# A two-layer graph network on one core: weight turned in the first linear, degree sums on VectorE, self part emptied by two engines

## What is computed

```python
deg     = segment_sum(ones, dst);  deg_inv = 1 / max(deg, 1)
mean(h) = segment_sum(h[src], dst) * deg_inv[:, None]
h   = relu(x @ W_self0 + mean(x) @ W_neigh0 + b0)
u   = h @ W_self1 + mean(h) @ W_neigh1 + b1
y   = layernorm(x + u)
# GCN: edges (row=src, col=dst) plus one self loop per node
g   = y @ W.T + b;   d = degree(row) ** -0.5
out = layernorm(y + segment_sum((d[row] * d[col])[:, None] * g[col], row))
```

## Time and profile before

| | |
|---|---|
| time, median of 3 runs | 850.34 us (850.06 to 852.06) |
| profiled execution, its own time | 849.59 us |
| its span, first to last instruction | 847.9 us, so 1.7 us lie around it |
| mean granted TensorE clock | 0.999 |
| TensorE busy | 830.6 us, 98% of the span |
| GpSimd busy | 459.1 us, to about 622 us |
| VectorE busy | 461.3 us |
| ScalarE busy | 177.4 us |
| DMA | 180.52 MB, 213 GB/s on average |

### The profile page before, as it was taken

How to read it: one execution, slowest core, us unless ns; L and a number is a source line. 1 busy time by engine, 2 the same in 40 slices (tenths; PEclk the granted TensorE clock), 3 DMA queues, 4 the chain that set the end, 5 groups by cost and what they waited for, 6 DMA issues and landing times.

```text
span 847.9 us, 11000 instructions
## 1 busy us (share of the span) xinstructions
PE 830.6 (98%) x4295; PEld 707.9 (83%) x4295; DVE 461.3 (54%) x714; ACT 177.4 (21%) x218; POOL 459.1 (54%) x343
## 2 busy tenths in 40 slices
PE   8999999999999999999999999999999999999996
PEld 6888888888897899788888888778889889988885
DVE  6465568200017565897544677775556435455555
ACT  4111132110111113353123112222222122200000
POOL 5028887787777887885888788788620000000000
PEclk9999999999999999999999999999999999999999
DMA  9977965463776425668876668267877649555551
GB/s 332 380 304 267 350 193 168 125 176 75 213 236 180 122 57 133 249 237 286 298 282 222 243 220 284 62 176 214 240 245 255 223 150 295 189 199 199 198 193 46
DMA packets 99480, 180.52 MB, mean 213 GB/s; under 512 B 15474, under 2 KB 75898, under 8 KB 94048
## 3 DMA queue, kind: packets, MB, share of 16 engines
q1 hardware_dynamic: 60144, 124.17, 44.0%
q10 hardware_dynamic: 26896, 40.65, 13.3%
q0 software_dynamic: 12384, 14.95, 7.6%
HBM read 107.08 MB, written 72.43 MB: 212 GB/s over the span
## 4 chain that ended last, share of the span: by engine, by line
PE 61%; POOL 15%; DMA 9%; issue 8%; DVE 5%; SPq 1%; ACT 1%; POOLq 0%; ACTq 0%; DVEq 0%
PE ps L1572 19%; POOL adj_in L643 14%; PE ps L1429 12%; PE ps L1606 10%; PE ps L1589 9%; PE ps L1515 8%; DMA adj_in<-u 4%; DMA first_rows<-in_L_gnn_W_neigh 1%; DMA spare<-in_x 1%; DMA xin<-s0t_scr 1%; PE ps L1413 1%; DVE u L914 1%; PE ps L1380 1%; SPq L514 1%; DVE sacc L1303 0%
## 5 line engine op out<-in xcount | busy, mean ns | idle before, releaser
L643 POOL DMA_INDIRECT adj_out<-loops,idx_out x160 | 245.2, 1533 | 65.4 <-issue 65.4
L643 POOL DMA_INDIRECT adj_in<-mult,idx_in x160 | 198.1, 1238 | 86.8 <-issue 86.8
L1572 PE MATMUL ps<-u 128*128 128x512 f32 x840 | 190.7, 389 | 1.4 <-DVE u L914 1.4
L1572 PEld LDWEIGHTS ps<-u 128*128 128x128 f32 x840 | 157.6, 188 | 34.2 <-issue 1.6
L1484 PE MATMUL ps<-wx 128*128 128x512 f32 (+1 forms) x576 | 109.4, 351 | 1.3 <-ACT outb L761 1.3
L1484 PEld LDWEIGHTS ps<-wx 128*128 128x128 f32 x576 | 93.9, 189 | 16.9 <-ACT outb L761 1.9
L1429 PE MATMUL ps<-u 128*128 128x512 f32 x432 | 98.2, 389 | 0.0
L1515 PE MATMUL ps<-wx,u 128*128 128x256 f32 (+5 forms) x640 | 94.8, 309 | 1.2 <-DVE ht L1191 1.2
L1589 PE MATMUL ps<-u,panel_tiles 128*128 128x512 f32 (+1 forms) x400 | 93.9, 393 | 1.9 <-DVE u L914 1.9
L1429 PEld LDWEIGHTS ps<-u 128*128 128x128 f32 x432 | 81.0, 188 | 16.8
L1515 PEld LDWEIGHTS ps<-wx,u 128*128 128x128 f32 (+1 forms) x640 | 86.6, 191 | 8.2 <-DVE ht L1191 1.6
(11 more groups left out here) (167 smaller groups left out, 779.8 us busy)
## 6 DMA issues: line engine op xcount, KB each, us to landing
left_scr<-u SPq DMA_DIRECT2D x7, 2560.0 KB, 9.5
u<-left_scr SPq DMA_DIRECT2D x7, 2560.0 KB, 9.6
xt_scr<-wx ACTq DMA_DIRECT2D x10, 1024.0 KB, 9.9
u<-xt_scr SPq DMA_DIRECT2D x10, 1024.0 KB, 5.1
wx<-xt_scr SPq DMA_DIRECT2D x16, 512.0 KB, 4.0
adj_in<-u POOLq DMA_DIRECT2D x4, 1600.0 KB, 25.3
adj_out<-u POOLq DMA_DIRECT2D x4, 1600.0 KB, 16.1
wx<-adj_in SPq DMA_DIRECT2D x5, 1280.0 KB, 7.1
```

What stands on the lines that cost most here:

```text
L643: pool.indirect_dma_start(table, bass.IndirectOffsetOnAxis(ap=index[0:EP, j:j + 1], axis=0), counts[0:EP, j:j + 1], None, bounds_check=CEL ...
L1572: ins = nc.tensor.matmul(ps[:, product_bank(g, i, p), :], left_op[n % 2][:, p, k, left, :], right_op[n % 2][:, k, right, :], start=(not on ...
```

## The change

1. The GCN weight is turned in the first linear: after steps 10 and 18 of tiles 5 to 8 instead of in mean1. Its loads stand in SyncE's queue between the loads of x tiles 6 to 9, its copies and stores in ScalarE's before the eviction of the tile. The loads of W_self0's first four row blocks then wait for the turning and for the stores.
2. The degrees of mean0's chunks 0 and 1: VectorE sums the 10 panels elementwise (`colsum`), and TensorE needs one matmul against ones instead of ten. It is issued after block 0 of chunk 0 and after block 3 of chunk 1. Chunks 2 and 3 keep theirs.
3. The tiny matmuls of L1522 go. The inverse degrees go through DRAM (dinv_scr): four small stores, one load before mean1.
4. Self part: ScalarE empties the even blocks, VectorE the odd ones, into 8 places; ScalarE issues all stores. The fetches of blocks 0 to 3 are issued during the last chunk of the self part.
5. The tables are cleared from a run of zeros that is a quarter as long, read four times, so four times as many pieces; adj_out is cleared after the first put. Some semaphores are merged, and b1 is loaded after mean0's last degrees.

```diff
@@ SyncE
             for t in range(2, NT):
                 load_x(t)
+                if t in (6, 7, 8, 9):
+                    for k in (2 * t - 12, 2 * t - 11):
+                        sp.wait_ge(w_lo_done, KD * S0)
+                        if k >= 2:
+                            sp.wait_ge(wt_turned, k - 1)
+                        sp.dma_start(raw[:, k % 2, :], w_gcn[k * P:(k + 1) * P, :]).then_inc(wt_in[k % 2], 16)
             for k in range(4):
-                sp.wait_ge(w_lo_done, KD * S0)
+                if k < 2:
+                    sp.wait_ge(wt_turned, 7 + k)
+                else:
+                    sp.wait_ge(wt_stored[k % 2], 16 * KD // 2)
                 load_w(S0, k)
...
+                if i == 20:
+                    sp.wait_ge(xt_turned, NT)
+                    for m in range(4):
+                        fetch_self(m)
...
+                if d == 6:
+                    t0, n = CHUNKS[c]
+                    sp.wait_ge(dinv_row_done, c + 1)
+                    sp.dma_start(dinv_scr[lines(CHUNKS[c])].rearrange("(a j) -> a j", a=1), dinv_row[0:1, c % 2, 0:n * T]
+                                 ).then_inc(dinv_stored[c % 2], 16)
...
@@ GpSimd
-                runs = table.rearrange("(p a j) o -> a p (j o)", a=4, j=ZERO_RUN)
+                runs = table.rearrange("(p a i j) o -> a p i (j o)", a=4, i=ZERO_TIMES, j=ZERO_RUN)
                 for a in range(4):
-                    pool.dma_start(runs[a, :, :], zeros).then_inc(done, 16)
+                    pool.dma_start(runs[a, :, :, :], zeros.unsqueeze(1).broadcast_to([P, ZERO_TIMES, ZERO_RUN])).then_inc(done, 16)
...
-                        if (g, c) == (0, RUN // 2) and not general_form:
+                        if (g, c) == (0, 0) and not general_form:
                             clear(adj_out, cleared_out)
...
@@ ScalarE
+            def keep_turned(k):
+                act.wait_ge(wt_turned, k + 1)
+                if k >= 2:
+                    act.wait_ge(wt_stored[k % 2], 16 * (k // 2))
+                else:
+                    act.wait_ge(w_lo_done, KD * S0)
+                nc.scalar.activation(outb[:, k % 2, :], pair_bank(3), ACT.Copy).then_inc(wt_copied, 1)
...
-            for i, (c, d) in enumerate(S0_BLOCKS):
+            for i, (c, d) in list(enumerate(S0_BLOCKS))[0::2]:
...
-                nc.scalar.activation(staged[i % 4][:, 0:width], ps[:, d, 0:width], ACT.Identity, bias=b0c[:, d:d + 1]).then_inc(s0_free, 1)
+                nc.scalar.activation(staged[i % 8][:, 0:width], ps[:, d, 0:width], ACT.Identity, bias=b0c[:, d:d + 1]).then_inc(s0_free[0], 1)
...
@@ VectorE
+            for i, (c, d) in list(enumerate(S0_BLOCKS))[1::2]:
+                dve.wait_ge(s0_full, i + 1)
...
+                nc.vector.tensor_scalar(staged[i % 8][:, 0:width], ps[:, d, 0:width], b0c[:, d:d + 1], None, ALU.add).then_inc(s0_free[1], 1)
...
                 if d == 0:
+                    if c < 2:
+                        dve.wait_ge(m1_full[c], 16 * n // 2)
+                        nc.vector.tensor_reduce(sacc[:, 0:width].rearrange("p (n j) -> p n j", n=n // 2),
+                                                m1_panels[c][:, :, :, :].bitcast(F32).rearrange("p k n j -> p n j k"), AX_X, ALU.add
+                                                ).then_inc(colsum_done, 1)
+                        dve.wait_ge(colsum_done, 2 * c + 1)
+                        nc.vector.tensor_copy(colsum[:, 0:width], sacc[:, 0:width]).then_inc(colsum_done, 1)
                     dve.wait_ge(deg_full, c + 1)
...
@@ TensorE
+                    if q == N0 and t in WEIGHT_TILES and i in (10, 18):
+                        turn_weights(2 * t - 10 + (i == 18))
...
+            def degrees(c, width, exact):
+                pe.wait_ge(*s0_bank_free(6 + c))
+                pe.wait_ge(colsum_done, 2 * c + 2)
...
+                    ins = nc.tensor.matmul(bank, ones_r[:, :], colsum[:, 0:width], start=True, stop=True)
+                ins.then_inc(deg_full, 1)
...
-                        if d == 2:
-                            pe.wait_ge(dinv_row_done, c + 1)
-                            for i in range(n):
-                                ins = nc.tensor.matmul(ps[:, 6 + c % 2, i:i + 1], dinv_row[0:1, c % 2, i * T:(i + 1) * T],
-                                                       ones_nt[0:1, 0:1], start=True, stop=True)
-                            ins.then_inc(dcol_full, 1)
+                        if (c, d) in ((0, 0), (1, 3)):
+                            degrees(c, width, exact)
...
-                        if 1 <= t <= KD:
-                            turn_weights(t - 1)
```

More of the change, by code:

```diff
@@ L92, in build @@
         base = -(-nc.sbuf_base // 32) * 32
[L93 removed]
+        U_AT, WX_AT, R_AT, E_AT, B_AT, END = (base + n for n in (0, 81920, 163840, 188416, 197120, 201216))
         sb("arena", [P, (END - base) // 4], F32)
@@ L213, in quarter @@
             return buf.rearrange("p a d -> p (a d)")[:, j * BANK:j * BANK + WIDE]
-        staged = [quarter(outb[:, :, :], j) for j in range(4)]
+        staged = [quarter(buf, j) for buf in (outb[:, :, :], raw[:, :, :]) for j in range(4)]
         fetched = [quarter(xin[:, :, :], j) for j in range(4)]
@@ L457, in load_chunk_1 @@
                     sp.wait_ge(h_full, KD * (c - 1))
-                    sp.wait_ge(dsum_done, sum(n for _, n in CHUNKS[:c - 1]) // 2)
+                    sp.wait_ge(dsum_done, sum(n for _, n in CHUNKS[:c - 1]))
                 for b in range(c + 1):
@@ L524, in _ @@
             for j in range(4):
-                sp.wait_ge(s0_stored[j], 16 * 6)
+                sp.wait_ge(s0_stored[j], 16 * 3)
             load_block(0, 1, 0)
+            for s in range(2):
+                sp.wait_ge(dinv_stored[s], 16 * 2)
+            sp.dma_start(dinv[:, :], dinv_scr.rearrange("(t p) -> p t", p=P), allow_slow_non_contiguous=True).then_inc(dinv_in, 16)
+            sp.wait_ge(deg_full, 4)
+            sp.dma_start(bias[:, :], b1.rearrange("(a d) -> a d", a=1).broadcast_to([P, D])).then_inc(bias_full, 16)
             sp.wait_ge(h_sum, KD * 4)
@@ L566, in _ @@
             sp.dma_start(bias[:, :], b_gcn.rearrange("(a d) -> a d", a=1).broadcast_to([P, D])).then_inc(bias_full, 16)
-            for s in range(2):
-                sp.wait_ge(wt_stored[s], 16 * KD // 2)
             load_w(GCN, 0)
@@ L1375, in turn_weights @@
                 if c == 0:
-                    pe.wait_ge(*summed(1, 6, 2))
+                    pe.wait_ge(flag_ready, 1)
+                    pe.wait_ge(b0c_ready, 1)
                 else:
@@ L1492, in typed @@
                 return ap.bitcast(F32) if exact else ap
+            def degrees(c, width, exact):
+                pe.wait_ge(*s0_bank_free(6 + c))
+                pe.wait_ge(colsum_done, 2 * c + 2)
+                bank = ps[:, 6 + c % 2, 0:width]
+                if exact:
+                    ins = nc.tensor.matmul(bank, ones_r[:, :].bitcast(F32), sacc[:, 0:width], start=True, stop=True)
+                else:
+                    ins = nc.tensor.matmul(bank, ones_r[:, :], colsum[:, 0:width], start=True, stop=True)
+                ins.then_inc(deg_full, 1)
             def mean0(exact):
@@ L1498, in mean0 @@
                     pe.wait_ge(m1_full[c], 16 * n // 2)
-                    if c < 2:
-                        pe.wait_ge(s0_free, s0_bank_free(6 + c))
-                    else:
-                        pe.wait_ge(dcol_read, c - 1)
-                    for k in range(NT):
-                        ins = nc.tensor.matmul(ps[:, 6 + c % 2, 0:width].rearrange("p (n j) -> p n j", n=n // 2), typed(ones_r[0:rows(k), :], exact),
-                                               typed(panels[0:rows(k), k, :, :], exact), start=(k == 0), stop=(k == NT - 1))
-                    ins.then_inc(deg_full, 1)
+                    if c >= 2:
+                        pe.wait_ge(deg_read, c - 1)
+                        for k in range(NT):
+                            ins = nc.tensor.matmul(ps[:, 6 + c % 2, 0:width].rearrange("p (n j) -> p n j", n=n // 2),
+                                                   typed(ones_r[0:rows(k), :], exact), typed(panels[0:rows(k), k, :, :], exact),
+                                                   start=(k == 0), stop=(k == NT - 1))
+                        ins.then_inc(deg_full, 1)
                     for d in range(KD):
```

128 lines of the change are left out of this document (64 added, 64 removed).

## The result

| | before | after |
|---|---|---|
| time, median us (8 runs each, side by side) | 851.29 | 857.57 |
| ratio of times | | 1.0091, 95% interval 1.0076 to 1.0106 |
| profiled execution: span us, mean granted clock | 847.9, 0.999 | 855.5, 0.991 |

What follows compares the result with a forecast made beforehand. TensorE, 98% busy, was taken as the bound. Its terms sum to -10.1 us, but new waits and GpSimd's chain leave the gather 2.1 earlier; less 0.2 for the clock, -1.9 on 850.34 gives 848.4 us, range 844.0 to 855.0.

Steps and rivals of the forecast that it cites:

- The savings on TensorE: Work and waits removed from TensorE in mean1, self part, degrees and tiny matmuls: 8.1, 1.3, 1.1 + 3.4 and 2.5 us.
- the chain of GpSimd: Puts, last panel load and gather: the gather starts at 633.2, against 632.9 by TensorE, hiding 0.3 us of clock loss.
- Mean1 and turning in mean1: Mean1 without turning the weight takes 92.0 us instead of 100.1: a gain of 8.1.
- Self part: TensorE's waits for banks that come free late in the self part go: a gain of 1.3 us.
- Third new wait: Before mean0's chunk 2: panels load late behind chunk 1's late degree and VectorE's sums, 5.2 us, bounds 3 and 8.
- Turning in the first linear: Eight groups of transposes moved into the first linear, 0.79 us each: 6.3 us more on TensorE.
- 1 us of wait before the self part: Self part's first loads stand behind the last turned block's store: 1 us late, bounds 0 and 8.
- First new wait: After block 0 of mean0's chunk 0, TensorE waits for VectorE's degree sum: 1.5 us, bounds 0 and 3.
- The clock: Slower TensorE clock after the wait at chunk 2: possible cost 0 to 2 us, taken as 0.2 net.
- Nothing before the products: No change forecast in TensorE's wait between mean0 and the products.
- GpSimd's last put: Last put, gating the gather, moves 2.5 us later through slower clears, with -3 and +11.3 as ends.
- savings 7.0 forecast: In mean0: degrees of chunk 0 (1.1 us) and chunk 1 (3.4), and tiny matmuls removed (2.5).

Runs made afterwards that it cites:

- the second pair: The unaltered kernels before and after, run and profiled once more: 850.25 us beside the after run's 856.66, ratio of after 1.0074.
- r_after: The changed kernel again, unaltered: 856.66 us, ratio 1.0074 to the kernel before.
- e1: Changed kernel with the degrees of chunks 0 and 1 summed by TensorE's ten matmuls again, on a slower chip: ratio 0.9958 to the kernel before.
- e10: Changed kernel with chunk 2's panels asked for before block 12's self part is fetched: 851.39 us, ratio 0.9999 to the kernel before.
- r_before: The kernel before again, unaltered: 849.8 us, ratio 0.9992.
- e9: Changed kernel with 16 filler matmuls in TensorE's wait for chunk 0's degree: 851.29 us, ratio 1.0024 to the kernel before.
- e13: Changed kernel with turning back in mean1, chunk 0's degrees on TensorE, chunk 2's panels asked for earlier, clears as before: 849.03 us, ratio 0.9995 to the kernel before.
- e12: Kernel before with the change's self part alone, clears as before: 847.23 us, ratio 0.9974 to the kernel before.
- e14: Changed kernel with chunk 0's degrees on TensorE, chunk 2's panels asked for earlier, clears as before: 852.73 us, ratio 1.004 to the kernel before.
- e11: Changed kernel with the two clears as in the kernel before: 864.51 us, ratio 1.0175 to the kernel before.
- e16: Kernel before with the changed self part, clears as before, and reciprocal roots brought into columns by memory, on a slower chip: ratio 0.994 to the kernel before.
- e7: Changed kernel with turning back in mean1, chunk 0's degrees on TensorE, chunk 2's panels asked for earlier: 854.5 us, ratio 1.0061 to the kernel before.
- e15: Kernel before with the changed self part, clears in long pieces, the second after the first put, on a slower chip: ratio 0.9992 to the kernel before.
- e6: Changed kernel with the tiny matmuls for the reciprocal roots back: 858.43 us, ratio 1.0082 to the kernel before.
- e2: Changed kernel with chunk 2's panels asked for before the fetch of block 12, on a slower chip: ratio 0.9944 to the kernel before.
- e5: Changed kernel with chunk 0's degrees on TensorE and chunk 2's panels asked for earlier: 850.86 us, ratio 0.9986 to the kernel before.

## Why the prediction was wrong

The savings on TensorE came out as forecast. What failed are prices: turning in the first linear (7.3 with its wait, measured 9.5), the strided sum behind the first wait (1.5 us of wait, measured 4.4), the clock (0.2, measured about 5), and the chain of GpSimd that should have hidden part of it and hid nothing. Term by term:

- **Mean1 and turning in mean1, -8.1**: right (-8.2). **Self part, -1.3**: right (-1.0; 2.2 to 2.4 in the second pair).
- **Third new wait, 5.2 before chunk 2**: right in cause and size (4.8; 5.2 in r_after). e1 and e10 take it away from either side.
- **Turning in the first linear, +6.3, with 1 us of wait before the self part**: mis-sized. A group of transposes costs (13.60 - 11.79) / 2 = 0.91 us, not the 0.79 between two starts, which left out its last overlap: 7.2. With 0.8 of wait for ScalarE's store, 0.7 before the self part and 0.4 from the first tiles, it makes 9.2 of the 9.55 measured. The wait before the self part was right.
- **First new wait, chunk 0's degree, 1.5**: failed at "reads 2560 elements, as the reduction of 2.81 us does". The strided sum took 4.52, and the wait was 4.4, past my upper bound of 3. The sum explains 1.7 of the 2.9 that I missed. Most of the rest is VectorE's start: 1.9 us after block 0's first matmul (247.88 - 245.95), where I had 0.5, because its last self block came late; in e10 it started 0.6 after, and the wait was 3.15. The Trainium skill (SBUF — State Buffer, Door 1: The DMA port swizzle) says that consecutive accesses within one line of 16 bytes run at full rate and each crossing pays; the row above is in line with it, 1.6 times the contiguous one; no run separates the stride from the number of results, 256 a partition instead of 10.
- **The clock, "I take 0.2 net"**: failed. Chunk 2 took 335.49 - 313.12 = 22.4 us, against 321.73 - 300.62 - 0.5 of tiny matmuls = 20.6 in r_before: 1.8. Chunk 0 cost 1.5 (e9). The products, 192.3 from first matmul to last against 190.7 in r_before: 1.6. Together about 5 us in the profiled execution, of which 1.1 comes off again before mean1 (0.82 of wait there instead of 1.94). I had weighed only the wait at chunk 2, at 0 to 2 us, and taken almost none of it.
- **Nothing before the products**: failed. The wait there was 1.43 in the trace of before, over ScalarE and VectorE, not TensorE; taking 0.6 of tiny matmuls out of chunk 3 could only lengthen it. It was 3.3 in one profile and 1.6 in the other, so the 0.1 belongs to the program and 1.7 to the execution. What makes the difference is not settled: VectorE takes chunk 3's second block 5.8 us after TensorE's first matmul of the blocks in the first profile (342.38 - 336.60) and 4.7 in r_after (341.65 - 336.99), but TensorE's rows give 18.03 us for the 160 matmuls in both.
- **GpSimd's last put, +2.5, hiding part of all this**: failed both ways. In the changed kernel it was not later (618.85), so the gather started when TensorE came, 642.95, with nothing hidden: the sum on TensorE is the result. And the forecast looked at the puts only at the gather. They also gate chunks 2 and 3 of mean0, with 2.4 us of slack at chunk 3, as e13 and e12 show.

In mean0 the terms are then: savings 7.0 forecast, 7.4 by e14 (6.3, and 1.1 for the ten matmuls that it keeps); waits 9.2 (4.4 and 4.8) instead of 6.7; clock 3.3 instead of 0.2; about 1.9 more before the products. -7.4 + 9.2 + 3.3 + 1.9 = 7.0, against +6.7 measured. So the savings were right, and what was missed is what the waits cost.

The change as a whole: turning early takes 9.5 to give 8.2, and forces the clear forward (e11, e14). The degrees on VectorE save TensorE's time, but in mean0 the chains of VectorE and GpSimd then set when it may go on. What pays is part 4 alone (e12, 0.26% faster). Part 3 with it (e16, 0.6%) was measured only on a chip whose ratios do not carry over; whether it adds anything is open.

## What to carry to other kernels

Before counting matmuls saved, list for each later load which chain issues it, and its slack at every one of those points, not only at the last: here 2.4 us at one chunk decided what a 6 us saving was worth. A new wait on TensorE costs its length and, in each of the cases from 3.0 us on seen here, the half clock behind it, 1.5 to 2.7 us; so two waits of 4.5 cost at least 12. Shorter waits may cost it too (1.8 us in e7). An edit that looks like housekeeping (where a table is cleared) needs an experiment of its own; two parts of a change can be tied together by nothing but the traffic they send at the same time.

## What the runs showed of the hardware

- The 24 waits of 3.0 to 10.6 us on TensorE in these profiles all had a granted clock of 0.50 behind them, most for 3 to 5 us of work. The clock fell at several shorter ones too: 1.4 (e16), 1.7 (e15), 1.8 (e7), 2.2 (e6) and 2.4 us (e2). It stayed at 1.00 at others of like length: 1.6 before the products in r_after, 1.9 before mean1 in the kernel before, 2.6 in the first linear of e2. The length of the wait alone does not tell which. The price was 1.5 us (chunk 0, e9) to 2.7 (e5, the gather's first 160 matmuls in 22.09 instead of 19.42).
- The same 100 matmuls of chunk 3 took 11.43 us in e12 and 15.38 in e15, at a granted clock of 1.00 in both. On the two chips where before takes 871 us many blocks of 256 and 226 columns in mean0 are longer in this way (not all: e15's chunk 2 takes 7.36 and 12.26 as in the kernel before), with pauses of 0.16 to 0.35 us that are put down to "issue"; the stages with 512 columns differ by about 1%. What slows them there is not known. First e12, then e15:

```profile
327.88 11.43 PE L1562 MATMUL ps<-wx,u 128*128 128x226 f32 x100
```

```profile
342.44 15.38 PE L1562 MATMUL ps<-wx,u 128*128 128x226 f32 x100
```

- GpSimd's puts pause now and then for 2.3 to 8.7 us with nothing awaited in the program. With one clear of 6.55 MB seven puts further forward such a pause stood at 124 us, where the DMA engines were full, and not at 137 (e15 against e12 and e16), and took 6.5 us instead of 2.3. In r_after, with the clear as early, it took 3.8.
